# Differential attention in a post-norm decoder: four key banks in one run, values behind the scores, output product among the next keys

## The reference, cut to what matters

```python
q, k, v = (x @ W).reshape(B, S, 2, 16, 64)  # for each of Wq, Wk, Wv: two attentions
s1, s2 = q1 @ k1.T * scale, q2 @ k2.T * scale      # causal, per head
a1, a2 = softmax(s1), softmax(s2)
lam = exp(lq1 . lk1) - exp(lq2 . lk2) + 0.8
o = (a1 @ v1 - lam * a2 @ v2) * (1 - 0.8)
x = layernorm(x + o @ Wo)
```

## Time and profile before

| | us |
|---|---|
| runs before | 1658.73, 1660.99, 1661.41 (median 1660.99) |
| profiled execution, its own time | 1658.21 |
| its span | 1656.5 |
| TensorE busy in the span | 1577.7 (95%), granted clock 0.991 |
| VectorE / ScalarE / GpSimd busy | 1232.4 / 918.1 / 676.5 |
| key matmuls of this phase (L1486) | 256.4 |

### The profile page before, as it was taken

One profiled execution on the slowest core, in us unless ns is written; L12 is line 12 of the kernel. 1 busy time (PEld: TensorE's weight loads), 2 busy tenths in 40 slices (PEclk: granted clock), 3 DMA queues, 4 the chain that ended last, 5 costly groups with the idle time before them and its releaser, 6 DMA issues. The chain is left out here.

```text
span 1656.5 us, 51937 instructions
## 1 busy us (share of the span) xinstructions
PE 1577.7 (95%) x18069; PEld 1327.1 (80%) x18069; DVE 1232.4 (74%) x3513; ACT 918.1 (55%) x2620; POOL 676.5 (41%) x1068
## 2 busy tenths in 40 slices
PE   7999999999999999999999999899999999999795
PEld 5887788787777777777777777799999999999664
DVE  6889888676777777677777776578888888888654
ACT  5777777643544444554445544566666666666241
POOL 3666655412333333333333333234444444444346
PEclk9999999999999999999999999999999999999897
DMA  3214221121220001111000000121212212122231
GB/s 106 65 48 120 71 57 56 45 60 51 51 54 26 25 25 30 27 29 28 25 25 25 25 26 27 40 59 45 62 47 56 60 43 62 48 56 58 71 113 40
DMA packets 157654, 82.30 MB, mean 50 GB/s; under 512 B 17641, under 2 KB 153115, under 8 KB 157568
## 3 DMA queue, kind: packets, MB, share of 16 engines
q1 hardware_dynamic: 154800, 77.68, 17.5%
q0 software_dynamic: 2048, 3.15, 0.6%
q10 hardware_dynamic: 720, 0.33, 0.1%
HBM read 61.03 MB, written 21.27 MB: 50 GB/s over the span
## 5 line engine op out<-in xcount | busy, mean ns | idle before, releaser
L1486 PE MATMUL bank<-diff_xT,diff_w_score 128*128 128x128 f32 x2048 | 256.4, 278 | 0.7 <-ACT diff_xT L1603 0.7
L1486 PEld LDWEIGHTS bank<-diff_xT,diff_w_score 128*128 128x128 f32 x2048 | 238.7, 192 | 22.4 <-issue 20.2
L1610 ACT ACTIVATE diff_keys<-bank 128x512 f32<-128x512 f32 x256 | 152.3, 595 | 161.7 <-PE bank L1486 161.7
L2085 ACT ACTIVATE lat_prob<-bank,lat_neg_max 128x128 f32<-128x128 f32 x512 | 180.6, 367 | 81.2 <-DVE lat_neg_max L2239 79.6
L1800 POOL TENSOR_TENSOR diff_prob<-diff_prob,diff_inv_sum 128x512 f32<-128x512 f32 x64 | 67.1, 1049 | 369.4 <-DVE diff_inv_sum L1703 369.4
L2301 POOL TENSOR_TENSOR lat_prob<-lat_prob,lat_inv_sum 128x512 f32<-128x512 f32 x128 | 133.4, 1042 | 131.5 <-DVE lat_inv_sum L2217 130.6
L2010 PE MATMUL bank<-lat_catT,lat_query 128*128 128x128 f32 x1024 | 139.3, 279 | 4.7 <-ACT lat_query L2096 4.7
L1978 PE MATMUL bank<-lat_catT,lat_w_score 128*128 128x128 f32 x1024 | 138.6, 279 | 3.8 <-issue 2.5
L1988 PE MATMUL bank<-lat_probT,lat_c_rep 32*128 32x256 f32 x2048 | 121.2, 384 | 14.9 <-DVE lat_z L2222 14.6
L1998 PE MATMUL bank<-lat_w_vo,lat_ctxT 128*128 128x128 f32 x1024 | 130.3, 275 | 1.1 <-ACT lat_ctxT L2108 1.1
L2010 PEld LDWEIGHTS bank<-lat_catT,lat_query 128*128 128x128 f32 x1024 | 125.3, 193 | 6.4 <-ACT lat_query L2096 5.1
(11 more groups left out here) (274 smaller groups left out, 3678.1 us busy)
## 6 DMA issues: line engine op xcount, KB each, us to landing
lat_c_rep<-cat SPq DMA_DIRECT2D x128, 128.0 KB
stage<-low_y SPq DMA_DIRECT2D x64, 64.0 KB, 1.6
diff_x_rep<-stage SPq DMA_DIRECT2D x128, 32.0 KB, 1.7
lat_c_t<-cat SPq DMA_DIRECT2D x32, 128.0 KB, 2.1
exp_w<-in_L_ffn_w_dram SPq DMA_DIRECT2D x16, 256.0 KB
expert_rows<-latw_zeros SPq DMA_DIRECT2D x4, 548.0 KB, 5.5
exp_rows<-expert_rows SPq DMA_DIRECT2D x8, 274.0 KB
low_x_t<-in_x_dram SPq DMA_DIRECT2D x32, 64.0 KB, 1.8
```

Of the source, the lines that this page charges most:

```text
L1486: last = nc.tensor.matmul(ring[(k + d) % 2][:, j * P:(j + 1) * P], w_score[:, H1 * (k // 2) + HS * d + 4 * (k % 2) + j, :], xT[:, :], star ...
L1610: nc.scalar.activation(keys[:, k // 2, 4 * (k % 2):4 * (k % 2) + 4, :].rearrange("p h t -> p (h t)"), ring[(k + d) % 2][:, :], ACT.Copy).t ...
L2085: last = nc.scalar.activation(prob[:, q, m, :], ps_s[q][:, m * T:(m + 1) * T], ACT.Exp, bias=neg_max[:, q, m:m + 1], accum_out=row_sum[:, ...
```

## The change

The diff, with the unchanged surroundings cut:

```diff
         ps_mix = core.bank[4:8]
+        key_banks = [ps_mix[0], ps_mix[1], ring[0], ring[1]]
...
+        def out_bank(i):
+            return ring[1] if isinstance(i, int) and i == NPAIR + 1 else ps_mix[2]
...
# TensorE, transpose_x
                 wait(pe, k_copied, 8 * i)
+                wait(pe, o_copied, 2 * i - 3)
...
-            def key_bank(n, d, k, ready, count):
-                wait(pe, ready, count)
+            def key_bank(d, k):
                 for j in range(4):
-                    last = nc.tensor.matmul(ring[(k + d) % 2][:, j * P:(j + 1) * P],
+                    last = nc.tensor.matmul(key_banks[k][:, j * P:(j + 1) * P],
...
# TensorE, scores: the two mask matmuls become a function of their own, masks()
...
# TensorE, pair
                         if d == 0:
                             pe.wait_ge(xT_ready, i + 1)
-                            key_bank(n, d, 0, k_copied, 4 * n)
-                            key_bank(n, d, 1, z_done, i - 1)
-                        else:
-                            key_bank(n, d, 0, k_copied, 4 * n)
-                            key_bank(n, d, 1, o_copied, n - 2)
+                        key_bank(d, 0)
+                        key_bank(d, 1)
+                    if d == 0 and have(i, 2):
+                        pe.wait_ge(o_copied, 2 * (i - 1))
+                        for t in range(HS):
+                            last = nc.tensor.matmul(out_bank(i)[:, 0:D], oT[:, t // 4, t % 4, :], wo[:, t, :],
+                                                    start=(t == 0), stop=(t == HS - 1))
+                        last.then_inc(wo_done, 1)
+                    if have(i):
+                        if d == 1:
+                            wait(pe, o_copied, n - 2)
+                        key_bank(d, 2)
+                        if d == 0:
+                            wait(pe, o_copied, n - 2)
+                        key_bank(d, 3)
                     if have(i, 1):
                         pe.wait_ge(rep_loaded[1 - par], ...)
+                        if have(i):
+                            pe.wait_ge(k_copied, 4 * n + 2)
+                        if d == 0:
+                            wait(pe, z_done, i - 1)
                         mixes(n - 2, d, 1 - par)
...
                     if have(i):
-                        key_bank(n, d, 2, k_copied, 4 * n + 1)
-                        key_bank(n, d, 3, k_copied, 4 * n + 2)
+                        scores(n)
                     if have(i, 1):
-                        if have(i):
-                            pe.wait_ge(k_copied, 4 * n + 3)
                         values(n - 2, d)
...
                     if have(i):
-                        scores(n)
+                        masks()
                     if d == 1 and more(i):
                         transpose_x(i + 1)
-                    if d == 1 and have(i, 1):
-                        (wait for o_copied 2 * i, the eight matmuls with wo into ring[1], wo_done)
...
# ScalarE, pair: copy_keys 2 and 3 move from behind the mix copies to ahead of them
...
# VectorE, pair: sums_low moves from behind the mix copies to directly behind sums;
# the sum z (d == 0) moves from ahead of sums to behind sums_low, and reads out_bank(i)
```

More of the change, by code:

```diff
@@ L1533, in scores, with masks @@
                                      start=True, stop=False)
+            def masks():
                 mask = tri[:, None, :].to_broadcast([P, HS, L])
@@ L1561, in pair @@
                     if have(i):
-                        key_bank(n, d, 2, k_copied, 4 * n + 1)
-                        key_bank(n, d, 3, k_copied, 4 * n + 2)
+                        if d == 0:
+                            pe.wait_ge(tri_done, 4)
+                            pe.wait_ge(ffn.z_done, ffn.NG)
+                        scores(n)
                     if have(i, 1):
-                        if have(i):
-                            pe.wait_ge(k_copied, 4 * n + 3)
-                        else:
+                        if not have(i):
                             wait(pe, o_copied, n - 3)
@@ L1572, in pair @@
                     if have(i):
-                        if d == 0:
-                            pe.wait_ge(tri_done, 4)
-                            pe.wait_ge(ffn.z_done, ffn.NG)
-                        scores(n)
+                        masks()
                     if d == 1 and more(i):
                         transpose_x(i + 1)
-                    if d == 1 and have(i, 1):
[L1581 to L1585, removed]
             pe.wait_ge(early.loaded[2], early.all)
@@ L1610, in copy_keys @@
                 nc.scalar.activation(keys[:, k // 2, 4 * (k % 2):4 * (k % 2) + 4, :].rearrange("p h t -> p (h t)"),
-                                     ring[(k + d) % 2][:, :], ACT.Copy).then_inc(k_copied, 1)
+                                     key_banks[k][:, :], ACT.Copy).then_inc(k_copied, 1)
             def exps(n, d, part):
@@ L1630, in pair @@
                         exps(n - 1, 1 - d, 1)
+                    if have(i):
+                        copy_keys(n, d, 2)
+                        copy_keys(n, d, 3)
                     if have(i, 1):
@@ L1640, in pair @@
                         latent.copies(act, (0, 1) if d == 0 else (4, 5))
-                    if have(i):
-                        copy_keys(n, d, 2)
-                        copy_keys(n, d, 3)
                     if have(i, 1):
@@ L1710, in pair @@
                         shift(n - 1, 1 - d)
[L1711 to L1716, removed]
                     if d == 1 and have(i, 2):
@@ L1723, in pair @@
                         sums(n - 1, 1 - d)
+                        sums_low(n - 1, 1 - d)
+                    if d == 0 and have(i, 2):
+                        dve.wait_ge(res_loaded, 16 * (i - 1))
+                        dve.wait_ge(wo_done, i - 1)
+                        nc.vector.scalar_tensor_tensor(out=z[:, :], in0=out_bank(i)[:, 0:D], scalar=1.0 - LAMBDA,
+                                                       in1=x_res[:, :], op0=ALU.mult, op1=ALU.add).then_inc(z_done, 1)
                     if have(i, 1):
@@ L1731, in pair @@
                                 .then_inc(mix_dve, 1)
-                    if done:
-                        sums_low(n - 1, 1 - d)
                     if d == 0:
```

## The result

| | before | after |
|---|---|---|
| runs, us | 1658.73 to 1661.41 (4) | 1676.65, 1682.97, 1683.0, 1683.23 |
| median | 1660.74 | 1682.99 |
| profiled execution, its span, granted clock | 1658.21, 1656.5, 0.991 | 1683.23, 1681.5, 0.986 |

The change makes the kernel slower: ratio 1.0104, interval 1.0069 to 1.0138. The forecast was 1679.0, with 1666 to 1689 as its range. The whole interval lies above 1, though the change is small. One execution of the kernel before, among those beside experiments 5, 6, 8 and 9, took 1983.18 us at a mean granted clock of 0.749, and no ratio uses it.

What follows compares the result with a forecast made beforehand. TensorE was taken to bound the kernel, busy for all 19.8 us of a pair. Terms -4.3 + 21.6 + 1.6 = +18.9 us gave 1677.1 on the profiled execution, 1679 stated for the median; range 1666 to 1689.

Steps and rivals of the forecast that it cites:

- the sum: Whole kernel: -4.3 + 21.6 + 1.6 = +18.9 us; 1677.1 on the profiled execution, 1679.9 on the median, stated as 1679.
- Part 1: Keys entered once per step, mixes and scores adjacent: mixes start 3.67 us behind the first key.
- Part 2: Values behind scores wait 0.14 us a step for mix copies, 3.08 behind mixes; key run gains only 0.14 a pair, -4.3.
- Part 3: Wo product leaves the pair's end, uncovering the copy of x: 0.72 us a pair, 30 times, +21.6 us.
- Part 4: Added waits, such as mixes for key copy 1 and z, are free; z has 1.2 us to spare at d = 0.
- Part 5: At i = 32 no keys cover z: mixes about 4.2 us behind the masks; +1.6 us once, between 0 and 2.2.
- The rule weighed: VectorE's first mix copy of d = 1, beside POOL's multiplication, is not held since it reads PSUM; no time added.
- Rival B: VectorE's mix copy is held by POOL or something else in its new place: +9 us, about 1688; chance 0.08.
- A: Rival: stop at the pair's end is smaller or values do not wait: 8.7 us less, about 1670; chance 0.12.
- C: Rival: copy of x at the pair's end is hidden after all, about 1656 to 1658; chance 0.06.
- D: Rival: fewer shape changes on TensorE save over 0.43 us a step, kernel faster; at 0.6 about 1645; chance 0.07.

Runs made afterwards that it cites:

- Experiment 5: Changed kernel with four of the eight Wo matmuls put behind the transpose at the pair's end, the other four left among the next keys; median 1655.14 us, ratio 0.9973.
- Experiment 6: Changed kernel with the whole Wo product back at the pair's end, behind the transpose; median 1690.89 us, ratio 1.016.
- 8: Changed kernel with the transposed x copied twice, first to a spare tile; runs 1682.04 and 1688.51 us, ratio 1.0127.
- 9: Kernel before the change with the transposed x copied twice, first to a spare tile; median 1660.43 us, ratio 0.9993.
- experiment 2: Changed kernel with the next x transposed between scores and values and copied ahead of the copy to oT; median 1658.37 us, ratio 0.9974.
- 3: Changed kernel with the two mask matmuls between scores and values, transpose still last; median 1684.57 us, ratio 1.0129.
- 4: Changed kernel with masks and, at d = 1, the transpose between scores and values, x copied ahead of oT; median 1659.56 us, ratio 0.9985.
- 7: Experiment 6 with TensorE's wait for z taken last of those ahead of the mixes of d = 0; one run, 1684.26 us.
- 5 again: Experiment 5 unedited, run again beside the versions with a rewritten end; median 1657.77 us, ratio 0.9979 to the kernel before.
- 2 with the new end: Experiment 2 with the last Wo products sent to ring[1], so mixes at i = 32 need not wait for z; median 1655.48 us, ratio 0.9956.
- 1: The changed kernel run again without edit; median 1679.12 us, ratio 1.0093 to the kernel before.
- 5 with the new end: Experiment 5 with the last Wo products sent to ring[1], so mixes at i = 32 need not wait for z; median 1655.24 us, ratio 0.9962.

## Why the prediction was right

The side and the size were right, and so was the cause. That the second sample's median, 1679.12, meets the forecast of 1679 this closely is in part luck: the sum was about 1 us too high, it had been rounded down from 1679.9, and a median depends on how many of its runs had the fallen clock. By its steps:

- **Part 1, the run of keys.** Mixes 3.67 behind the first key: measured 3.67. With the pair's end repaired (experiment 2) the loop gains 0.15 a pair; the step said 0.14.
- **Part 2, values.** 3.08 behind the mixes: measured 3.07 in both steps. The table of waits names ScalarE's half of the mix copies as the releaser of the weight load, but that half ends at 712.49 and VectorE's at 712.69, 0.14 ahead of the values at 712.83. At d = 0 it is 0.14 behind VectorE again (703.82 to 703.96), and so it is at i = 32, where TensorE stands idle for 0.47 ahead of the values (1047.33 to 1047.47). That VectorE's copy sets them rests on these rows; no experiment moved that copy.
- **Part 3, the pair's end.** Masks to keys 0.95 and 0.10 for the first pass: measured 0.95 and 2.05 instead of 1.95. That ScalarE's order (`oT` first) delays the copy of x as in the earlier trace rows was right too: it starts 0.39 behind the transpose. Experiments 2, 5, 8 and 9 show the cause from four sides. The parts add up to a period of 19.79 - 0.14 + 0.72 = 20.37; measured 20.35.
- **Part 4, waits.** Free in the changed kernel: z ends at 719.92, 4.24 behind the first key, and the mixes start at 5.56. But the step didn't say what its 1.2 us of slack rest on: the Wo product among the keys. Experiment 6 takes that product away and z holds the mixes. The product covers z in its new place as it had covered x in its old one. SyncE's loads of x for the mixes start 5.30 behind the first key (720.98), 1.7 later than before and not some 3.
- **Part 5, the end.** Mixes of i = 32 were to start about 4.2 behind the masks; they started 4.05 behind (1040.35 to 1044.40). From these masks to the second mixes 10.04 instead of 8.52: +1.5, said +1.6.
- **The rule weighed.** VectorE's mix copy of d = 1 takes 1.29 (711.40), though GpSimd multiplies until 711.63, the same 1.29 as at d = 0 (702.53) with no multiplication beside it; and the context rows' norm, now clear of GpSimd, takes 0.34 at 713.02 instead of 0.93. So the trace agrees with the Trainium skill ("SBUF — State Buffer", Who interferes with whom), over an overlap of 0.23 us. The sum z, which also reads PSUM, takes 0.29 at 719.63 with a multiplication of GpSimd beside it from 719.68, and 0.28 in the earlier trace rows with GpSimd idle. Rival B, a mix copy that is held, is out.

```profile
711.01 0.62 POOL L1815 TENSOR_TENSOR diff_prob<-diff_prob,diff_inv_sum 128x256 f32<-128x256 f32 x1
...
713.02 0.34 DVE L1766 TENSOR_SCALAR diff_ctx_n<-diff_ctx_t,diff_mean_var,diff_rstd 128x128 f32<-128x128 f32 x1
```

- **The sum.** +18.9 was forecast; the phase grew by 19.5 in the profiled executions, 1.56 of which is the first key block at a fallen clock (5.46 instead of 3.90). At like clocks the kernels differ by 17.6. So the sum is about 1 us too high, well within its bounds.
- **What the sum left out** is the clock. The median of 1682.99 lies 4 above the forecast, since three of its four runs had the fallen clock; the next sample of the same kernel gave 1679.12. The scatter was 2.8 in the runs I had, and I took it for the whole. The range also mixed two bases: +12 to +28 on the profiled 1658.2 is 1670 to 1686, on the median 1673 to 1689, and the stated 1671 to 1689 is neither; both hold the result.
- **Rivals.** A and C are out (values 3.07 behind the mixes, a stop at every pair). D's 0.43 a step from fewer changes of shape is not there: the step d = 1 takes 8.64 from keys to masks instead of 8.69.

## What to carry to other kernels

Work that could stand anywhere in an order may be what hides a short chain between two engines: before moving it, list what passes through other engines while it runs, at the place it leaves (here transpose, copy, first key) and at the place it goes to (here z). If a part of it is cover enough, move only the rest: half of the Wo product did both jobs. And where a wait really holds, take it last of those that stand together.

## What the runs showed of the hardware that had not been expected

- **The granted clock differs from execution to execution in code that is not changed.** Over 306 to 322 us the profiled executions show 1.00 (before, 5), 0.89 (3, 4, 6, 7, 8, and 5 again), 0.79 (9, and 2 with the new end), 0.52 (2) and 0.50 (after, 1, and 5 with the new end); at 0.50 the stretch runs at 1.2 GHz instead of 2.4. Experiment 5 was profiled twice and shows 1.00 and 0.89. Ahead of the stretch TensorE stops for 0.47 and 0.51 us (at 303 and 305 us), in the execution of before that keeps its clock as in that of after, which loses it. The mean clock of an execution goes with it: 0.990 or 0.991 where the stretch shows 0.89 or more, 0.985 or 0.986 where it shows 0.50. After's ten runs go by that mean: three at 0.991 near 1676, five at 0.986 near 1683, two between. What decides it is open.
- **A change of shape costs time that no idle shows.** Shape means here how many rows and columns of the array a matmul takes. The first fp32 key pass behind the values, which use 64-column groups, lost 0.10 us, and nothing with the two bf16 mask matmuls between (3.84 and 3.74 for the same 32 passes). Ahead of the values it is the other way round: the first value starts 0.20 behind the second mask (0.12 from mask to mask) and in experiment 2 0.26 behind the transpose (0.11 from pass to pass), so that with either between scores and values these start 3.25 and 3.19 behind the mixes instead of 3.07.
- **A releaser by the profile can be a bystander.** In experiment 6 the copy that happened to end last was named; moving the wait for z moved the start of the mixes from 4.50 to 4.17 behind the first key.
- **Waits behind a wait.** Of the 0.48 us between z and the mixes of that pair, 0.34 went when z was waited for last, with three waits fewer behind it. In the pairs of experiment 6 that are written out, where the values waited for are constants, it was 0.21 with the old order of waits (z ends at 1034.50, mixes at 1034.71). That the rest goes into working out the values in registers fits both, and was not tried by itself.
